# Loop heads of two cross attentions at the start of an instruction fetch block

## The reference, cut to what matters

```
# layer 0: 16 heads of 64; keys are the 257 context rows and the 32 latents
x = x + softmax(q @ k.T * 64**-0.5, masked) @ v @ Wout
# layer 1: 16 heads of 8; keys are the 257 context rows
x = x + softmax(q @ k.T / sqrt(8), masked) @ v @ W_o.T + b_o
# between and after them: a gated linear recurrence, a quantised FFN, a Fenwick-masked
# self attention and a mixture of 16 experts
```

## Time and profile before

| what | us |
|---|---|
| median of 3 runs | 2055.96 |
| lowest and highest | 2054.47 to 2059.80 |
| the profiled execution, its own time | 2053.8 |
| span from its first to its last instruction | 2051.7 |

### The profile page before, as it was taken

The page is one execution under the profiler, slowest core; times in us unless marked ns, Lnnn a source line. Parts: engine busy times, 40 slices in busy tenths (PEclk is TensorE's granted clock), DMA queues, the critical chain, the costliest instruction groups (busy, mean ns, idle before and its releaser), DMA issues. The chain is left out here.

```text
span 2051.7 us, 51500 instructions
## 1 busy us (share of the span) xinstructions
PE 1718.3 (84%) x13455; PEld 1392.9 (68%) x13455; DVE 1594.6 (78%) x4998; ACT 1504.4 (73%) x4156; POOL 908.9 (44%) x1339
## 2 busy tenths in 40 slices
PE   3599999999999999971710679999999799749997
PEld 3489999999999999941500356666667566427775
DVE  4798888888888888837788669999999588636664
ACT  3488888888888888854765479999999588545553
POOL 1544444444444444304156034444444377335554
PEclk8599999999999999995755799999999799879998
DMA  4277676777777777610000059999999300103322
GB/s 139 85 167 165 160 160 157 161 163 162 159 162 163 159 160 164 151 42 0 0 0 0 2 147 250 252 250 251 249 249 248 73 1 0 32 13 102 91 87 82
DMA packets 196234, 259.54 MB, mean 127 GB/s; under 512 B 25136, under 2 KB 141328, under 8 KB 196032
## 3 DMA queue, kind: packets, MB, share of 16 engines
q1 hardware_dynamic: 194678, 256.53, 50.0%
q10 hardware_dynamic: 1194, 1.58, 0.3%
q0 software_dynamic: 288, 0.56, 0.1%
HBM read 86.09 MB, written 4.72 MB: 44 GB/s over the span
## 5 line engine op out<-in xcount | busy, mean ns | idle before, releaser
L778 ACT ACTIVATE a_prob<-a_neg,a_nmax 128x289 f32<-128x289 f32 x512 | 266.6, 525 | 1.4 <-DVE a_nmax L705 1.1
L840 PE MATMUL a_out<-a_probT,a_xn 128*128 128x256 f32 x1024 | 263.0, 380 | 5.0 <-DMA a_probT<-a_blocks 4.2
L1710 ACT ACTIVATE b_prob<-b_neg,b_nmax 128x257 f32<-128x257 f32 x512 | 260.6, 515 | 6.9 <-DVE b_nmax L1661 6.8
L671 POOL TENSOR_TENSOR a_xn<-a_z,g 128x256 f32<-128x256 f32 x128 | 93.8, 733 | 384.6 <-DVE a_z L739 384.6
L830 PE MATMUL a_score<-a_xnT,a_qT 128*128 128x290 f32 x1536 | 252.9, 314 | 2.5 <-DVE a_qT L750 2.5
L705 DVE CUSTOM_DVE_ANT_0 a_neg<-a_score,a_bias 128x289 f32<-128x289 f32 x512 | 211.6, 458 | 41.2 <-PE a_score L830 36.8
L786 ACT ACTIVATE a_prob<-a_prob,a_rinv 128x289 f32<-128x289 f32 x512 | 231.3, 527 | 1.8 <-DVE a_rinv L755 1.7
L830 PEld LDWEIGHTS a_score<-a_xnT,a_qT 128*128 128x128 f32 x1536 | 222.3, 190 | 9.6 <-issue 3.3
L1661 DVE CUSTOM_DVE_ANT_0 b_neg<-b_score,b_bias 128x257 f32<-128x257 f32 x512 | 188.6, 419 | 30.5 <-PE b_score L1801 15.3
L840 PEld LDWEIGHTS a_out<-a_probT,a_xn 128*128 128x128 f32 x1024 | 175.2, 191 | 19.8 <-DMA a_probT<-a_blocks 5.3
L716 DVE STREAM_TRANSPOSE a_blocks<-a_prob 128x1024 f32<-128x1024 f32 x128 | 159.4, 1245 | 24.0 <-ACT a_prob L786 17.7
(11 more groups left out here) (478 smaller groups left out, 4567.9 us busy)
## 6 DMA issues: line engine op xcount, KB each, us to landing
a_probT<-a_blocks SPq DMA_DIRECT2D x512, 192.0 KB, 3.6
b_probT<-b_blocks SPq DMA_DIRECT2D x256, 256.0 KB, 4.6
a_raw<-in_ctx SPq DMA_DIRECT2D x128, 128.0 KB, 2.9
b_raw<-in_ctx SPq DMA_DIRECT2D x64, 256.0 KB, 4.7
m_wide<-expert_weights SPq DMA_DIRECT2D x128, 128.0 KB, 2.9
a_kept<-keep SPq DMA_DIRECT2D x32, 257.0 KB, 3.4
b_kept<-keep SPq DMA_DIRECT2D x32, 257.0 KB, 4.8
b_v_rows<-ctx_tail_values SPq DMA_DIRECT2D x32, 256.0 KB, 4.7
```

What stands on the lines that cost most here:

```text
L778: nc.scalar.activation(prob[:, par, grp, 0:KEYS0], neg[:, grp, :], ACT.Exp, bias=nmax[:, par, grp:grp + 1], scale=-1.0, accum_out=rsum[:, ...
L840: nc.tensor.matmul(out_ps[:, half, 0:2 * P], xn[:, j, kt, :], probT[:, u, 2 * half:2 * half + 2, kt, :], start=(kt == 0), stop=False)
L1710: nc.scalar.activation(prob[:, (j + 5) % 4, grp, :], neg[:, par, grp, :], ACT.Exp, bias=nmax[:, par, grp:grp + 1], scale=-1.0, accum_out=r ...
```

## The change

One line of `run_steps`. [...] 

```
@@ -434,7 +434,7 @@
 
     for s in range(-lead, 8):
         step(s // 8, s % 8)
-    with eng.Fori(1, (B - rest) // 8) as g:
+    with eng.bass.Fori(1, (B - rest) // 8, engines=[eng.engine], head_slot={eng.engine: 0}) as g:
         for j in range(8):
             step(g, j)
     for s in range(B - rest, B + lag):
```

## The result

The changed kernel takes 2064.05 us (10 runs, 2061.22 to 2068.06), the kernel before 2056.88 us (10 runs beside them, 2053.53 to 2059.80): a ratio of 1.0038 with a 95% interval of 1.0027 to 1.0048, **7 us slower**.

The account below looks back on a forecast made before the run. TensorE was taken to bound loop one, with TensorE, ScalarE and the DMA engines all tight in loop two. Terms 0 + 0.1 + 0 + 1.2 + 0 gave +1.3 us: median 2057.3 us, range 2052 to 2063.

Parts of the forecast that it names:

- Inside the loops: In both loops' bodies and back edges: no instruction fetches to save and nothing added or removed, 0 us.
- The branches: Ahead of each loop: ten taken branches over never-executed padding, engines side by side, 0.1 us at most in the sum.
- What the branch can miss, loop one: At the entry of loop one: code that a branch might find not yet fetched, counted as 0 on the path.
- ScalarE at loop one: At loop one's entry: ScalarE's output copy about 1.6 us late for a code fetch, taken up by slack, 0 on the path.
- the worked bound of 1.2 us: At loop one's entry: TensorE would wait 1.2 us if the fetch delaying ScalarE's copy took 2.9 us.
- TensorE at loop two: At loop two's entry: branch about 17 slots into a block, next block still being fetched, TensorE stands 1.2 us, 0 to 2.5.
- After the loops: In all later code, shifted by up to a block: no refetches wherever it starts, 0 us, with ±1 us for chance.
- Rival A: At both loop entries: engines wait for target and next block, 2.9 and 4.7 us, nothing absorbed, +7.6 us, 2063.6; chance 0.06.
- Rival B: At VectorE's back edges: the aligned loop no longer fits and refetches, +40 us, or +10 at 0.42 us each; chance 0.02.
- Rival C: At VectorE's back edges in its 275-slot body: refetched today and not after, 40 us saved, 2016; chance 0.02.

Follow-up runs that it names:

- experiment 1: The change without TensorE's head in loop two and ScalarE's in loop one, eight heads aligned, against the kernel before: 2058.43 us, ratio 1.0008.
- experiment 7: Only ScalarE's head in loop one aligned, at slot 0, against the kernel before: 2055.86 us, ratio 1.0007.
- experiment 8: Only ScalarE's head in loop one placed, at slot 128, against the kernel before: 2057.27 us, ratio 1.0008.
- experiment 3: Only TensorE's two heads aligned, both at slot 0, against the kernel before: 2065.45 us, ratio 1.0034.
- experiment 5: Only TensorE's two heads placed, the first at slot 32, the second at slot 0, against the kernel before: 2061.47 us, ratio 1.0029.
- experiment 11: Only VectorE's head in loop one placed, at slot 111, against the kernel before: 2125.89 us, ratio 1.0347.
- experiment 4: Only TensorE's head in loop two aligned, at slot 0, against the kernel before: 2057.42 us, ratio 1.0005.
- experiment 6: Only TensorE's two heads placed, the first at slot 80, the second at slot 0, against the kernel before: 2058.81 us, ratio 1.0014.
- experiment 10: Only VectorE's head in loop one aligned, at slot 0, against the kernel before: 2058.85 us, ratio 1.0009.

## Why the prediction was wrong

- *Inside the loops: 0.* Right. The DMA views of the kernel after show no instruction queue from 206 to 846 nor from 1280 to 1570 us, and TensorE is busy for 646.00 of 646 us.
- *The branches: 0.1 us, padding nothing.* Right within what can be measured (experiment 1, eight of each: ratio 1.0008, 0.9999 to 1.0017).
- *What the branch can miss, loop one: 0.* For VectorE, GpSimd, SyncE and TensorE no run shows the term, since none shows where in its block each of their branches starts. What the runs showed in its place is no wait for issue of VectorE, GpSimd or SyncE between 147 and 200 us, nor one of TensorE at its entry.
- *ScalarE at loop one: 1.6 us, absorbed.* No row of the kernel before shows that its branch would miss. It did: experiments 7 and 8 tie the wait to the slot (2.14 us at slot 0, 0.19 at slot 128). The size was not right. It idled 2.55 us and its copy came 2.3 us late. Nor was it all absorbed: TensorE waited 0.62 us for the copy, and 0.60 us for VectorE, whose transposes ScalarE's normalisations had held up and whose 0.50 us of slack was to take this up. That the two make the worked bound of 1.2 us is chance; the bound was for a copy 2.9 us late and had only the first wait in it. I had taken the landing of 32 and 64 KB transfers of quiet stretches for a stretch in which the data queue is at 66.5%.
- *TensorE at loop two: 17 slots after the crossing, 1.2 us, 0 to 2.5.* **This is the step that failed.** The place was right, the wait shrinks with the counted distance as one for a fetch under way would (5.32 us at 17 slots, 3.05 at 49, none for code at 97), and experiment 3 puts the whole loss there. TensorE idled 5.0 us and not 1.2, since the fetch took over 5 us and not 1.6. The packet itself was as priced or somewhat longer (1.3 us here, 2.1 in experiment 3, against 0.85); what was missing is the time around it, 1.6 us from its end to the first load, and some 2 to 2.5 us until it moved (an estimate: 17 slots taken as 0.5 us ahead of the last values' end). The stage runs its DMA engines at 0.92, and 4.7 us, the landing in that very stage, stood in the earlier trace rows; I used it for rival A only. It came nearer than the nearest row in size. That the load is the reason is not shown: no run varied it.
- *What follows the gap* was missing altogether. TensorE came back from its 5 us at a granted clock of 0.50, here and in experiment 3, and that cost 2.7 us more. Gap and clock make 7.7 us where the sum had +1.2. After the gap of 3.05 us in experiment 5 the clock was 1.00.
- *After the loops: 0, ±1.* 0.8 us in the profile, within that. But the reason given, that position never costs, is false: experiment 11.
- *Rival A* (two entries at the loaded price, nothing absorbed, +7.6, 2063.6) came within half a microsecond of the median and had 0.06. That is partly luck. It had each entry wait for its code whatever the distance, and experiments 1, 4 and 6 show entries that do not; of its 2.9 us for stage one 1.6 reached TensorE, and its 4.7 us for stage two stand against a gap of 5.0 us and a clock that it did not have. *Rival B* did not happen at slot 0 (experiment 10), but a refetch in each iteration is what slot 111 shows, at 5 us an iteration and not 1.6. *Rival C*: nothing was there to save, since no instruction packet moved in the loop before. The loop of 275 slots moved none at slot 0 either, where by its count it touches three blocks of 8 KB, and five an iteration at slot 111, where it touches four.

## What to carry to other kernels

Before aligning a loop, look whether the trace has instruction packets inside it; if not, there is nothing to gain but safety, and of the ten loops one showed a need for it (275 slots: no packet in it at slot 0 and, by luck, none where it stood, and 70 us slower at slot 111). A branch into the next block waited for no code here when it came late enough in its own: count the slots from the start of the block in which the branch stands (97 were enough, 0.41 us ended by VectorE; 49 were not, 3.05 us), and price the fetch by transfers of the same stage, not by the quiet ones: 4.7 us came nearer to what was found here than 1.6. And one aligned loop sets where in its block the next one starts: the second head here was fine alone and cost 7 us behind the first.

## What the hardware showed that I had not expected

- A fetch of TensorE's code, in a stage with a DMA share of 0.92, kept its loads waiting 5.3 us when the branch came some 17 slots into the block, and not at all at 97 slots. The packet itself moved for 0.9 to 2.1 us of that, and the first load came 1.6 to 1.7 us after its end.
- The granted clock after an idle time of TensorE: 0.50 after 5.0 us (two traces), 1.00 after 2.8 us (one trace; 3.05 us ahead of its weight load), in the same place of the program.
- VectorE's loop with its head at slot 111 moved five 8 KB packets in each iteration (55 in 11), not one.
- No version tried beats the kernel before.
